# Decay attention in one hybrid kernel: key maxima per half of the queries, and packed rows written as blocks of 48 rows

## The reference, cut to what matters

```python
def _L1_attn_a_ref(x, W_q, W_k, W_v, W_o, W_down_kv, W_up_k, W_up_v):
    H, HD, LAMBDA_DECAY = 16, 8, 0.01          # x: (2, 1024, 128)
    q, k, v = x @ W_q, x @ W_k, x @ W_v
    latent_kv = (k + v) @ W_down_kv
    k_rec, v_rec = latent_kv @ W_up_k, latent_kv @ W_up_v
    # heads: (b, 16, 1024, 8)
    scores = einsum('bhqd,bhkd->bhqk', qh, k_rec) / sqrt(128)
    scores = scores * exp(-LAMBDA_DECAY * abs(t_q - t_k))
    attn = softmax(scores, axis=-1)
    return merge_heads(einsum('bhqk,bhkd->bhqd', attn, v_rec)) @ W_o
```

## Time and profile before

| | |
|---|---|
| time, median of 3 | 1208.28 us (1208.24 to 1210.48) |
| the profiled execution | 1208.88 us, its span 1207.1 us |
| TensorE | busy 1055.5 us, 87% of the span |
| VectorE | 761.0 us, 63% |
| ScalarE | 645.5 us, 53% |
| GpSimd | 185.6 us, 15% |
| 16 DMA engines | 31.95 MB, 26 GB/s over the span |

### The profile page before, as it was taken

How to read it: one execution, slowest core, us unless ns; L and a number is a source line. 1 busy time by engine, 2 the same in 40 slices (tenths; PEclk the granted TensorE clock), 3 DMA queues, 4 the chain that set the end, 5 groups by cost and what they waited for, 6 DMA issues and landing times.

```text
span 1207.1 us, 14239 instructions
## 1 busy us (share of the span) xinstructions
PE 1055.5 (87%) x5206; PEld 398.7 (33%) x5216; DVE 761.0 (63%) x1211; ACT 645.5 (53%) x1098; POOL 185.6 (15%) x107
## 2 busy tenths in 40 slices
PE   5899998975898888888888889998899747999998
PEld 2233343331233332333233223443343212334343
DVE  2677345277998988999896212014499998983200
ACT  4786454371067777777777773325763475412321
POOL 0222900032000000000000000000064323450000
PEclk8899998995589999999999999999899979999999
DMA  7000000134111110110000000000000000000000
GB/s 251 1 1 1 0 1 0 60 113 160 56 47 48 62 50 19 59 32 32 8 4 7 3 5 1 1 0 0 1 1 0 1 0 1 0 1 1 18 1 17
DMA packets 20763, 31.95 MB, mean 26 GB/s; under 512 B 6748, under 2 KB 14940, under 8 KB 20312
## 3 DMA queue, kind: packets, MB, share of 16 engines
q1 hardware_dynamic: 20696, 31.07, 7.5%
HBM read 23.23 MB, written 7.57 MB: 26 GB/s over the span
## 4 chain that ended last, share of the span: by engine, by line
PE 48%; ACT 14%; DVE 12%; issue 8%; POOL 1%; DMA 1%; SPq 1%; DVEq 0%; another core or an unknown queue 0%; POOLq 0%; ACTq 0%
PE PS L1419 17%; PE PS L1022 11%; ACT arena L1031 8%; PE PS L1006 5%; DVE SQ L919 4%; ACT arena L1037 3%; PE PS L1408 2%; PE PS L1428 2%; PE PS L1409 2%; DVE arena L1642 2%; PE PS L1063 1%; PE PS L909 1%; PE PS L1584 1%; PE PS L1594 1%; DVE arena L1525 1%
## 5 line engine op out<-in xcount | busy, mean ns | idle before, releaser
L1031 ACT ACTIVATE arena<-PS 128x384 f32<-128x384 f32 (+1 forms) x512 | 252.3, 551 | 142.5 <-PE PS L1006 142.0
L919 DVE CUSTOM_DVE_ANT_0 SQ<-PS,XP 128x1024 bf16<-128x1024 f32 x256 | 303.5, 1218 | 36.4 <-PE PS L909 36.3
L909 PE MATMUL PS<-arena 48*128 48x512 bf16 (+3 forms) x704 | 201.2, 356 | 20.4 <-DMA arena<-scr 13.0
L1006 PE MATMUL PS<-arena 50*128 50x512 bf16 (+3 forms) x640 | 153.2, 320 | 18.9 <-ACT arena L1031 11.2
L1022 PE MATMUL PS<-arena 128*32 128x512 f32 (+1 forms) x1280 | 137.4, 518 | 21.6 <-ACT arena L1037 20.7
L1419 PE MATMUL PS<-arena,w_h1T 128*128 128x512 f32 x256 | 118.0, 607 | 11.5 <-DVE arena L1457 6.6
L1447 ACT ACTIVATE arena<-PS,w_scl 128x512 f32<-128x512 f32 x64 | 43.7, 687 | 157.8 <-PE PS L1419 157.7
L1419 PE MATMUL PS<-arena,w_h2T 128*128 128x512 f32 x256 | 114.9, 594 | 0.0
L1006 PEld LDWEIGHTS PS<-arena 50*128 50x128 bf16 x640 | 42.8, 94 | 148.2 <-ACT arena L1031 141.1
L1642 DVE TENSOR_TENSOR_SCAN arena<-arena 128x512 f32<-128x512 f32 x64 | 83.1, 1298 | 0.1
L1671 POOL TENSOR_TENSOR arena<-arena 128x512 f32<-128x512 f32 x32 | 58.6, 1830 | 155.2 <-DVE arena L1650 155.2
(11 more groups left out here) (220 smaller groups left out, 1517.5 us busy)
## 6 DMA issues: line engine op xcount, KB each, us to landing
scr<-arena SPq DMA_DIRECT2D x16, 384.0 KB, 3.9
arena<-scr SPq DMA_DIRECT2D x64, 96.0 KB
arena<-scr SPq DMA_DIRECT2D x64, 64.0 KB
arena<-scr SPq DMA_DIRECT2D x64, 32.0 KB
XP<-xT SPq DMA_DIRECT2D x1, 1024.0 KB, 4.8
w_h1T<-h1T SPq DMA_DIRECT2D x1, 1024.0 KB, 6.6
w_h2T<-h2T SPq DMA_DIRECT2D x1, 1024.0 KB, 8.4
out_xT<-XR SPq DMA_DIRECT2D x4, 256.0 KB, 2.3
```

What stands on the lines that cost most here:

```text
L909: mm = t.matmul(PS[:, bank, k0 - lo:k1 - lo], packed(m, g, v, slice(q * P, (q + 1) * P), KP), packed(m, g, 2 + v, slice(k0, k1), KP), star ...
L919: v.tensor_tensor_reduce(JUNK[:, u % 2, :], PS[:, bank:bank + 2, :].rearrange("p a b -> p (a b)"), STRIP[:, at:at + S], 1.0, -3.0e38, ALU. ...
L1006: mm = t.matmul(PS[:, score_bank(T, i), at:at + b_ - a_], packed(n, g, 2 + v, slice(kt * P, (kt + 1) * P), KP + MROWS), packed(n, g, v, sl ...
L1031: nc.scalar.activation(PT[:, T % 2, score_head(T, i), a0_:a1_], PS[:, score_bank(T, i), a0_:a1_], ACT.Exp).then_inc(s_free, 1)
```

## The change

- **Maxima by halves.** A half is 512 queries: 4 tiles of each of 4 heads, NTH = 16 units. `unit_of` now gives first the 16 units of the first half of the queries, then those of the second. Copy, transpose, split and the 4 DMAs are made for each half, so 16 turns instead of 8, each with half the rows. `maxima_at(j)` is 8j - 5, and every eighth step waits for `pk_m`. The first turn comes after 16 units, so LEAD is 26, and the units are used up at T = 114; 13 steps are left without any.
- **The end.** PROJ_PE, LN5_AT, LAST_SUMS and the wait for the freed bank (SIXTH_FREE) are set to later step numbers, to fit into those 13 steps.
- **Packed rows.** `scr` now holds the six rows of each feature in their final order. A piece is stored as often as it is needed: hi three times, mid twice, lo once, by a repeated read, and each piece as soon as it exists (12 DMAs for a chunk instead of 4; twice the bytes). The read back is then 2 DMAs of 48 rows for a head, 8 for a group instead of 24. `PK` keeps the two halves of the queries apart.
- **Buffers.** The maxima and their copies have buffers of their own (MX, MXD, MH), the unneeded product goes to `ffn0`, and a memset of the old place is gone.

```diff
-        PK = place([NSLOT, 2, 4, S], BF16)
+        PK = place([NSLOT * 2, 2, 4, CH], BF16).rearrange("p (n e) f a t -> p n e f a t", e=2)
-        MXD = SQ[:, 0, 2 * P:3 * P]
-        JUNK = SQ[:, 2:4, :].rearrange("p a b -> p (a b)").bitcast(BF16).rearrange("p (a b) -> p a b", a=2)
-        MX = SQ[:, 0, 0:2 * P].rearrange("p (a b) -> p a b", a=2)
-        MH = SQ[:, 1, 0:2 * P].bitcast(BF16).rearrange("p (a k q) -> p a k q", a=2, k=2)
+        JUNK = ffn0[:, 0:S].bitcast(BF16).rearrange("p (a b) -> p a b", a=2)
+        MX = sb("MX", [P, 2, GH * NKT])
+        MXD = sb("MXD", [P, GH * NKT])
+        MH = sb("MH", [P, 2, 2, P], BF16)
-        scr = nc.dram_tensor("scr", (2, 3, B, P, 2, S), BF16).ap()
+        PIECE_ROWS = ((slice(0, 3), slice(4, 6), slice(3, 4)), (slice(2, 5), slice(1, 6, 4), slice(0, 1)))
+        scr = nc.dram_tensor("scr", (2, B, P, KP // HD, 2, 2, CH), BF16).ap()
-        PACKS = 6
+        PACKS = 2
+        STORES = 16 * 4 * 3
-        LEAD = NT1 + 10
+        NTH, KH = NT1 // 2, NKT // 2
+        LEAD = NTH + 10
...
-                    a.wait_ge(a1_stored[c % 2], 64)
+                    a.wait_ge(a1_stored[c % 2], STORES)
...
-        def maxima_at(m):
-            return NS * m - (LEAD - NT1) // 2
+        def maxima_at(j):
+            return NKT * j - (LEAD - NTH) // 2
         def unit_of(u):
             m, k = divmod(u, NT1)
-            return m, 2 * (k // 16) + 1 - k % 2, k % 16 // 2
+            hf, k = divmod(k, NTH)
+            pair, k = divmod(k, 2 * KH)
+            return m, 2 * pair + 1 - k % 2, KH * hf + k // 2
...
-        def both_sides_dve(v, m):
-            src = MX[:, m % 2, 0:NT1].rearrange("p (h v q) -> p h v q", h=GH, v=1).broadcast_to((P, GH, 2, NKT))
-            v.wait_ge(p1_free, NT1 * (m + 1))
+        def both_sides_dve(v, j):
+            m, hf = divmod(j, 2)
+            src = MX[:, m % 2, NTH * hf:NTH * (hf + 1)].rearrange("p (h v q) -> p h v q", h=GH, v=1).broadcast_to((P, GH, 2, KH))
+            v.wait_ge(p1_free, NTH * (j + 1))
...
+        TURNS = {maxima_at(j): j for j in range(1, 2 * NGRP)}
-                   PROJ_FROM + 3: ((1, 2), (1, 3)), NSTEP - 9: ((2, 0), (2, 1)), NSTEP - 4: ((2, 2),), NSTEP - 2: ((2, 3),)}
-        LAST_SUMS, LN5_AT = NSTEP - 7, NSTEP - 14
+                   PROJ_FROM + 3: ((1, 2), (1, 3)), NSTEP - 4: ((2, 0), (2, 1)), NSTEP - 3: ((2, 2),), NSTEP - 1: ((2, 3),)}
+        LAST_SUMS, LN5_AT, SIXTH_FREE = NSTEP - 4, NSTEP - 9, NSTEP - 4
...
+                if s % NKT == 0:
+                    t.wait_ge(pk_m, 64 * (T // NKT + 1))
                 if s == 0:
-                    t.wait_ge(pk_m, 64 * (n + 1))
...
-            v.wait_ge(a1_lo_free, 8 + 4 * (NCH - 1))
-            v.memset(SQ[:, 0, 0:3 * P], 0.0).then_inc(preload, 1)
-            v.wait_ge(preload, 1)
...
-                for v in range(4):
-                    sp.wait_ge(a1_lo_free, 8 + 4 * c + v + 1)
-                    dst = scr[v // 2, :, b, :, v % 2, j * CH:(j + 1) * CH].rearrange("k p t -> p k t")
-                    sp.dma_start(dst, SPL[c % 2][:, v, :, :]).then_inc(a1_stored[c % 2], 16)
+                for k in range(3):
+                    for v in range(4):
+                        rows = PIECE_ROWS[v // 2][k]
+                        if k == 0:
+                            sp.wait_ge(a1_hi, 4 * c + v + 1)
+                        elif k == 1:
+                            sp.wait_ge(a1_mid, 4 * c + v + 1)
+                        else:
+                            sp.wait_ge(a1_lo_free, 8 + 4 * c + v + 1)
+                        dst = scr[v // 2, b, :, rows, j, v % 2, :]
+                        sp.dma_start(dst, SPL[c % 2][:, v, k:k + 1, :].broadcast_to((P, 3 - k, CH))
+                                     ).then_inc(a1_stored[c % 2], 16)
             def packs(n):
                 for g in (1, 0, 3, 2):
+                    for side in range(2):
+                        dst = PK[row0(g):row0(g) + KP, n % NSLOT, side, :, g // 2 * 2:g // 2 * 2 + 2, :].rearrange("p f v t -> p f (v t)")
+                        sp.dma_start(dst, scr_heads[side, n, g]).then_inc(pk_in[n % NSLOT][g // 2], 16)
...
             maxima(0)
             packs(2)
             maxima(1)
             packs(3)
+            maxima(2)
             for n in range(NGRP - 1):
                 denominators(n)
+                maxima(2 * n + 3)
                 if n + NSLOT < NGRP:
                     sp.wait_ge(pv_free, NS * (n + 1))
                     packs(n + NSLOT)
                 reciprocals(n)
                 if n + 2 < NGRP:
-                    maxima(n + 2)
+                    maxima(2 * n + 4)
```

More of the change, by code:

```diff
@@ L747, in packed @@
         def packed(n, g, v, cols, rows):
-            return PK[row0(g):row0(g) + rows, n % NSLOT, v // 2, g // 2 * 2 + v % 2, cols]
+            hf = cols.start // CH
+            cols = slice(cols.start - hf * CH, cols.stop - hf * CH)
+            return PK[row0(g):row0(g) + rows, n % NSLOT, v // 2, hf, g // 2 * 2 + v % 2, cols]
         def key_tile(s):
@@ L968, in diag_pe @@
                     t.wait_ge(dg_free, d)
-                t.wait_ge(m_l, sum(maxima_at(m) < T for m in range(NGRP)))
+                t.wait_ge(m_l, sum(maxima_at(j) < T for j in range(2 * NGRP)))
             else:
@@ L1109, in a1_pe @@
                 u = LEAD + 2 * T
-                turn = n + 1 if n + 1 < NGRP and T == maxima_at(n + 1) else None
+                turn = TURNS.get(T)
                 def unit(k, half):
```

77 lines of the change are left out of this document (34 added, 43 removed).

## The result

| | before | after |
|---|---|---|
| median of the runs | 1209.12 us (1208.24 to 1210.48, 4 runs) | 1193.24 us (1193.0 to 1194.19, 4 runs) |
| the profiled execution, its span | 1208.88, 1207.1 us | 1193.0, 1191.2 us |

The forecast was -16.9 us in a range from 1185 to 1199.

The account below looks back on a forecast made before the run. VectorE bounds the lead, no engine is full in steps with units, ScalarE and TensorE share the bound without. Terms -7.5 - 19.1 + 23.5 + 4.4 - 18.2 = -16.9 us gave 1191.4 us; own range 1186 to 1196, with two rivals 1185 to 1199.

Parts of the forecast that it names:

- Start of the lead: Before the first unit: quicker packed reads start it at 277.0 instead of 284.54, -7.5 us.
- to each some 1.8 us from first issue to first data. I take the latter: First packs' landing: 2.6 us at 303 GB/s chosen over 9.7 us at 81 GB/s, plus 1.8, landed at 275.5.
- the rival of packs on few engines: Start of the lead: packs stay at 81 GB/s, first unit at 283.8, 1198.2 us; chance 0.12.
- Lead: Units ahead of the steps: 16 fewer at 1.193 us each, -19.1 us, T = 0 at 308.0.
- Both are in time, by 5 us: Before T = 0 at 308.0: first maxima landed at 302.9, SyncE free at 297, before the maxima's turn ends at 299.1.
- at 341 GB/s 23.1 us from 274: 297: SyncE's queue behind packs(0): 6.3 MB of stores and 1.57 MB of packs(1) done at 297.
- Steps with units and turns: Steps with units: 8 more steps, +23.5 us, and 8 more turns at 0.55 us each, +4.4 us.
- The rival of dearer turns: Turns cost 1.0 us instead of 0.55, 7.2 more; with the crowded end at most 1201.6 us, joint chance 0.10.
- Steps without units: After the last unit: 8 plain steps fewer, -18.2 us, projections, norm and sums staying in 12 steps.
- the rival of the crowded end: Last 12 steps cost 3 us more; with dearer turns +10.2, 1201.6 us at most, joint chance 0.10.
- The doubled stores as the bound: Stores and packs before the first maxima run at 170 GB/s, T = 0 at 343.3, 1226.7 us; chance 0.04.
- That the end doesn't follow: T = 0 comes early but something behind, such as TensorE's low clock, holds the pace: some 1210 us; chance 0.03.

Follow-up runs that it names:

- The halves alone: Kernel after, but pieces stored once and packs read as before, in 24 DMAs a group with repeated reads: 1209.93 us, ratio 0.9985.
- the three blocks: Kernel after, but each 48-row pack read in pieces of 24, 16 and 8 rows, nothing repeated: 1211.32 us, ratio 1.0003.
- the lead of 22: Kernel after with LEAD = 22, packs(1) ahead of the stores of the last two chunks, end items moved to fit: 1196.33 us, ratio 0.9889.
- The early order: Kernel after with LEAD still 26, SyncE issuing packs(1) and the first maxima ahead of stores(3): 1192.62 us, ratio 0.9863.
- the lead of 30: Kernel after with LEAD = NTH + 14 instead of NTH + 10: 1205.36 us, ratio 0.9958.
- the stores by version: Kernel after, but a chunk's 12 stores go out version by version, lo first, instead of by piece: 1200.27 us, ratio 0.9943.
- the packs alone: Kernel before (LEAD 42, maxima by whole groups) with only the new scr, stores and 48-row packs: 1204.77 us, ratio 0.9947.

## Why the prediction was right

**The mechanism and the size.** The mechanism held: quicker packs start the lead earlier, a lead of 16 units fewer shortens it, and steps and turns take their price back. Each term came out within 1.6 us of what was said (the first within 1.9, once the 1.0 us of upstream is taken off), and the sum within 1.0. "277.0 instead of 284.54" became 277.96; "26 x 1.193" became 31.18; T = 114 was to stand at 651.8 and stood at 652.66. That the sum came so near is in part luck: the start and the steps without units fell short by 1.9 and 1.6, and upstream, the stretch behind T = 126 and the rest, all put at nothing, gave 1.0, 1.1 and 0.3.

**Start of the lead.** The step that was wrong is "to each some 1.8 us from first issue to first data. I take the latter", with the 303 GB/s of a table load of 128 rows. The 48-row packs ran at 175 GB/s (196 KB every 1.13 us), and from the first issue to the fourth landing (269.70 to 276.78) passed 7.1 us instead of 4.4. The middle of the two bounds, 81 and 303, would have been nearly right. The 2.7 us cost the first unit 1.0 only, because the stores had landed at 269.63, not 271.1 (1.0 of this is upstream's), and the steps behind the landing took 0.3 less. VectorE's own preparation ended at 275.73, so it was not yet "the limit" that the prediction made it: the 2.23 us that it idles are what quicker packs could still give.

By the Trainium skill, "DMA: Bandwidth & Descriptors", section "Why a DMA increments its semaphore by 16 and not by 1", the engines of such a DMA are the largest number up to 16 that divides the slowest dimension of both sides, which makes 16 for 48 rows. The trace agrees: the window's share went from 0.23 to 1.03. That left the rival of packs on few engines without its ground; but 16 busy engines at 194 GB/s also show that the number of engines does not give the rate.

**Lead.** -18.9 for -19.1. But "Both are in time, by 5 us" failed. SyncE reached the maxima as they became ready; the landing was up to 6.5 us instead of 1.9, and the last came at 308.04 instead of 302.9. The term that was mis-sized is "at 341 GB/s 23.1 us from 274: 297". It gave packs(0) no time behind 274, though their last read landed at 281.25; and it priced packs(1) at the stores' rate, 4.6 us, where they took 9.0 (the last store landed at 297.57, the last read of packs(1) at 306.55, at 180 GB/s in the window above). The stores between went quicker than said, at some 380 GB/s. The margin left was 0.3 us, so that T = 0 was on time is luck. The halves alone, the three blocks and the lead of 22 show what happens when it goes: 8.5, 13.8 and 5.5 us in the first pair. The early order shows that in the kernel after it was not yet used up.

**Steps with units and turns.** +27.7 for +27.9. Turns at 0.57 us each and plain pairs at 5.75, so the choice to give nothing back for the halved rows held: VectorE's cast takes 0.28 us on 32 rows (L949), as it did on 64 (L941). By the prediction's own sign ("if pairs with turns exceed 6.5 us") one pair, 6.59 at T = 50, was over. The rival of dearer turns fell with this for T = 8j - 5. At T = 8j - 7 (the lead of 30) turns do cost more at the end of a group, but by the meeting with GpSimd's product, and not by the wait for `pk_m` that the rival had in mind.

**Steps without units.** -16.6 for -18.2. The term left out the clock. TensorE in the kernel after, four matmuls of the projections at each level:

```profile
666.53 1.98 PE L1071 MATMUL PS<-arena,w_wo 128*128 128x512 f32 x4
...
690.34 3.72 PE L1071 MATMUL PS<-arena,w_wo 128*128 128x512 f32 x4
```

The same projections take 3.72 us for 1.98. What the fall costs can be read from the three blocks: the same order of the end, but the clock held, and T = 114 to T = 126 takes 44.3 us for 47.2. So the 7 us at the low level cost 2.9 (an estimate from two kernels); without them the term would have been -19.5. The kernels with the norm one or two steps later took 43.1, 43.1 and 43.04, -20.7. So the projections and the norm do lie beside one another better in 12 steps than in 20, and that gain was eaten here; the 3 us that the rival of the crowded end named did come, and only 1.6 of them show because the rest of the term was 1.3 better than said. The order doesn't decide by itself whether the clock falls: of the traces with the order of after it fell in the kernel after, the halves alone, the early maxima, the lead of 30 and the stores by version, and held in the three blocks; with the order of before it held in before and fell in the packs alone. What makes it fall stays open.

**The other rivals.** The doubled stores as the bound are out: 384 GB/s in the window of stores above, and T = 0 on time, if by 0.3 us. (The rival's 14.1 MB is one group of packs short: four chunks of 3.15 MB and two groups of 1.57 make 15.7.) That the end doesn't follow is out as well, since the clock rose at 315.0, 5.9 us after T = 0, and before at 341.2, 6.6 after it. A last slip of the sums: the forecast's own range added up goes down to 1191.4 - 4.4 - 3 = 1184.0, not 1186.

## What to carry to other kernels

When a small transfer releases a step, count two queues ahead of it: the issues on its engine and the bytes already handed to the DMA engines. Price each kind of those bytes by its own rate (here 384 GB/s for stores and 180 for packs, with the same engines busy). Put the small transfer ahead of bulk that isn't due yet; only then a shorter lead counts (here 4 units: 4.7 us of lead, some 3.8 by T = 114). To see whether a step waited, look at the instruction that waits, not at a neighbour that marks the step. And a change that moves a small instruction in time has to be looked through for what another engine does just then.
